# A narrower span of nodes per tile of edges in a graph-network kernel: 12 nodes in place of 16

## The reference

```
xs = s @ W1_s / sqrt(64);  xv = einsum('nmc,mk->nkc', v, W1_v) / sqrt(32)
w  = silu(edge_embed @ fc_w1 + fc_b1) @ fc_w2 + fc_b2          # 192 weights per edge
m0_a = w_ss * xs[src] * sh0          m0_b = w_vv * einsum('emc,ec->em', xv[src], sh1) / sqrt(3)
m1_a = (w_sv * xs[src]) x sh1        m1_b = w_vs * xv[src] * sh0
agg = segment_sum(msg, dst, num_segments=n) / sqrt(AVG_DEG)
out = agg @ W2 + own features @ Wsc, gated by silu, added to the node features
```

## Time and profile before

| | us |
|---|---|
| median of three runs | 550.05 |
| the profiled execution's own time | 550.69 |
| its span, first to last instruction | 549.0 |
| gathers (L535) issued from, to | 41.2 to 535.5 |
| PE busy (at a mean granted clock of 0.936) | 474.3 |
| POOL busy (gaps between gathers not counted) | 401.4 |
| DVE busy | 368.0 |
| ACT busy | 202.1 |

### The profile page before, as it was taken

How to read it: one execution, slowest core, us unless ns; L and a number is a source line. 1 busy time by engine, 2 the same in 40 slices (tenths; PEclk the granted TensorE clock), 3 DMA queues, 4 the chain that set the end, 5 groups by cost and what they waited for, 6 DMA issues and landing times.

```text
span 549.0 us, 16081 instructions
## 1 busy us (share of the span) xinstructions
PE 474.3 (86%) x5423; PEld 354.2 (65%) x5423; DVE 368.0 (67%) x1234; ACT 202.1 (37%) x412; POOL 401.4 (73%) x429
## 2 busy tenths in 40 slices
PE   6839778889898999989899899899899989899896
PEld 5735555667665766667576667666666756676675
DVE  7945575666677587667667666676577667667664
ACT  4654422333343334333334334343243334334331
POOL 7737777777777777777777777777777777777770
PEclk9978699899899799989989899899799989989998
DMA  9982222222222222222222222222222222222220
GB/s 223 393 259 71 69 71 71 64 67 80 76 74 68 76 72 69 74 76 76 66 76 76 72 66 74 77 67 75 76 72 68 73 76 73 69 76 76 65 75 24
DMA packets 35374, 48.06 MB, mean 88 GB/s; under 512 B 9748, under 2 KB 27955, under 8 KB 34843
## 3 DMA queue, kind: packets, MB, share of 16 engines
q0 software_dynamic: 19968, 34.11, 22.8%
q1 hardware_dynamic: 14977, 13.65, 8.4%
q10 hardware_dynamic: 410, 0.07, 0.1%
HBM read 39.60 MB, written 4.00 MB: 79 GB/s over the span
## 4 chain that ended last, share of the span: by engine, by line
POOL 56%; issue 19%; PE 11%; DVE 4%; DMA 1%; DVEq 1%; ACT 0%
POOL gath L535 56%; PE ps L824 3%; PE ps L834 2%; PE ps L811 1%; DMA gath<-table,src_sb 1%; DVE P L645 1%; PE ps L829 1%; PE ps L801 1%; PE ps L866 1%; DVE agg L683 1%; DVE raw_stats L713 1%; DVE P L640 0%; PE ps L859 0%; DVEq L668 0%; PE ps L830 0%
## 5 line engine op out<-in xcount | busy, mean ns | idle before, releaser
L535 POOL DMA_INDIRECT gath<-table,src_sb x392 | 375.2, 957 | 126.1 <-issue 117.0
L834 PE MATMUL ps<-S,P 128*64 128x32 f32 x2496 | 172.2, 228 | 0.0
L829 PE MATMUL ps<-S,P 128*64 128x48 f32 x832 | 121.2, 241 | 52.5 <-DVE agg L683 50.5
L824 PE MATMUL ps<-fc_sb,hid 128*128 128x384 f32 x416 | 161.4, 513 | 0.0
L834 PEld LDWEIGHTS ps<-S,P 128*64 128x64 f32 x2496 | 160.3, 143 | 0.0
L829 PEld LDWEIGHTS ps<-S,P 128*64 128x64 f32 x832 | 82.1, 139 | 114.4 <-DVE agg L683 74.2
L640 DVE TENSOR_TENSOR P<-ps,gath 128x512 f32<-128x512 f32 x103 | 71.2, 691 | 114.2 <-PE ps L824 66.2
L568 ACT ACTIVATE hid<-ps,fb_sb 128x256 f32<-128x256 f32 x104 | 49.2, 473 | 195.3 <-PE ps L811 133.6
L683 DVE TENSOR_TENSOR agg<-ps,agg 128x64 f32 x412 | 91.4, 222 | 27.3 <-DVE agg L683 0.3
L830 PE MATMUL ps<-S,P 128*64 128x16 f32 x832 | 105.5, 205 | 0.0
L645 DVE TENSOR_TENSOR P<-ps,gath 128x384 f32<-128x384 f32 x206 | 104.2, 548 | 0.0
(11 more groups left out here) (118 smaller groups left out, 347.5 us busy)
## 6 DMA issues: line engine op xcount, KB each, us to landing
gath<-table,src_sb POOLq DMA_INDIRECT x392, 2.5
agg<-zeros SPq DMA_DIRECT2D x4, 1024.0 KB
out<-res SPq DMA_DIRECT2D x24, 78.1 KB
x_sb<-x SPq DMA_DIRECT2D x5, 350.0 KB
emb<-emb_t SPq DMA_DIRECT2D x104, 16.0 KB
table<-prod SPq DMA_DIRECT2D x3, 420.0 KB
sh_sb<-sh_t SPq DMA_DIRECT2D x1, 840.0 KB
raw<-x,src_sb POOLq DMA_INDIRECT x24, 6.5
```

Of the source, the lines that this page charges most:

```text
L535: nc.gpsimd.indirect_dma_start(gath[:, u, j, :], None, table, bass.IndirectOffsetOnAxis(ap=src_sb[:, t:t + 1], axis=0)).then_inc(arrived, 16)
L824: ins = nc.tensor.matmul(w_ps(u)[:, 2 * g:2 * g + 2, 0:WN], hid[:, u % 2, g, :], fc2_sb[:, :, :], start=False, stop=True, skip_group_check ...
L829: nc.tensor.matmul(oj[0:64, :, 0:3], pj[:, 64:128], sj[:, :, 1:4], start=True, stop=True)
L834: ins = nc.tensor.matmul(oj[64:128, :, c:4:3 - c], pj[:, lo:lo + 64], sj[:, :, 0:2 + c:1 + c], start=(c == 0), stop=(c == NC - 1), skip_gr ...
```

## The change

A single constant is changed: the span of nodes that a tile of edges adds into.

```diff
--- before.py
+++ after.py
@@ -22,7 +22,7 @@
-WIN = 16
+WIN = 12
```

## The result

The changed kernel took 546.14 us (median of 6, 545.27 to 546.94) against 549.93 us (median of 6). The ratio is 0.993, with a 95% interval of 0.9918 to 0.9943. The forecast was 547.9, with a range from 546.2 to 550.0: the sign and the place were right, the gain of 3.8 us is 1.7 times the 2.2 forecast, and the time lies just under the range.

What follows compares the result with a forecast made beforehand. POOL's gathers were taken to bound the kernel. From 550.69 us profiled, 1.7 for the gathers and 0.5 for the tail leave 548.5; the same step from the 550.05 median gives 547.9, range 546.2 to 550.0 for 8 in 10.

Steps and rivals of the forecast that it cites:

- What bounds the kernel: Main part: POOL's gathers are the time, 392 x 1.246 = 488 us; POOL never really waits for products.
- How much goes: Gathers in the main part: shorter selectors and matches hold gathers up less, 1.7 us gained; bounds 3.7 gained, 2.3 lost.
- (a): POOL's gathers: each of 23 hold-ups stays, its selector ending 84 ns sooner relative to the gather; 1.8 us gained.
- (b): POOL's gathers: selectors fall on gathers at random; 25 hold-ups of 3.7 us become 19 of 2.2; 1.5 us gained.
- phase lock: Rival, main part: one selector per iteration settles just ahead of a gather; 1.8 us slower, 551.9 us; chance 3%.
- best case: Gains' bounds: all selector hold-ups gone, 3.7 us, plus 0.8 us in the tail, give 545.6 us.
- VectorE per quad: Main part: shorter match, selector and additions take 0.15 us less per quad on VectorE, hidden by the gathers.
- TensorE per quad: Scatter matmuls with fewer columns: 0.15 us less per quad; 0.21 by the slope, nothing if weight loads set the pace.
- Tail: After the last gather: scatter and VectorE work on the path get shorter, 0.5 us gained; bounds 0 and 0.8.
- No change: Rival: hold-ups do not shrink and only the tail's 0.5 us is gained, 549.6 us, from 548.95 up; chance 23%.
- Two passes: Rival: a tile spanning more than 12 nodes runs the main part twice, near 1050 us; chance under 1%.
- TensorE's clock: Rival: TensorE idles more, its granted clock falls and it no longer keeps up; about 580 us at 0.70; chance 2%.

Runs made afterwards that it cites:

- Sel_wide: Against the kernel before: span 12 in matmuls and additions, matches and selectors still 16 wide; ratio 0.9983.
- order16: The kernel before with the selector moved from after the first to after the third of a quad's additions; ratio 0.9963.
- order12: The changed kernel (span 12) with the selector after the third addition in place of the first; ratio 0.9968 to the kernel before.

## Why the prediction was right, and where it failed

**What bounds the kernel:** right. POOL's gathers set the pace, TensorE's 86% did not matter, and no gather waited for products. The mean gather fell to 948 ns (952 forecast), and the last one ended at 531.6 us (533.8).

**How much goes: wrong, and this is the failed step.** The term was 1.7 us, between (a), 23 hold-ups that stay and shrink by 0.08 us, and (b), a random phase with 19 left of 0.116 us. Measured: 7 (in the second profile 1) left, 3.0 us gone from selectors, 3.65 us in all from the gathers. Method (b) gave 25 and 3.7 us for the kernel before where the trace has 23 and 3.7; I took the match as support for a random phase, and the experiments don't bear it out. Sel_wide, order16 and order12 have 16, 12 and 19 where it says 25, 25 and 19; two profiles of one kernel have 23 and 24. The hold-ups of most kernels repeat in one slot of the loop instead, and the changed kernel's selectors lie elsewhere. Method (a) moved the selector's end by 84 ns relative to the gather; in the quad shown it moved by 0.22 us, since the instructions ahead of it moved too. I had that argument in the text, against the phase lock ("that slot waits for TensorE's weights, which come earlier now"), and did not carry it into the sum. The forecast's best case, 3.7 us from selectors and 0.8 from the others, held what was measured. That the new place is a cheap one was luck as far as the sum goes: nothing in it put the selectors there, and order12, with the same lengths, settled elsewhere.

**VectorE per quad:** right (0.15 us). **TensorE per quad:** wrong, 0.15 us taken, 0.01 us measured (none from start to start); the three forms' durations with 48, 32 and 16 columns (241, 228, 205 ns) had suggested a price per column that the pace of the stream doesn't have. The lower bound that I named, nothing, is nearer; that the weight loads set the pace, the reason beside it, is not tested.

**Tail:** taken 0.5, measured 0.8 us, within the bounds, for partly other reasons. In the first pair of profiles the products of the last whole quad start 2.50 us after their last gather was issued, where it was 2.75, and wait for its landing. The timeline of after:

```profile
526.87 0.95 POOL L535 DMA_INDIRECT gath<-table,src_sb  x1 [0.30 <-issue]
...
529.37 0.69 DVE L640 TENSOR_TENSOR P<-ps,gath 128x512 f32<-128x512 f32 x1 [1.72 <-DMA gath<-table,src_sb]
...
537.31 0.21 DVE L690 TENSOR_TENSOR agg<-ps,agg 128x48 f32 x1 [0.20 <-PE ps L834]
```

From there to the first of the last additions it is 6.73 in place of 6.94 us, as VectorE's columns say (0.22 forecast). The four last additions take 1.42 in place of 1.71, because the third no longer waits 0.4 us for TensorE. 0.25 + 0.21 + 0.29 = 0.75. The last of the three can't be put down to the change: in the second profiles the kernel before has no such wait (1.51) and the changed one has it (1.67), and there the tail is 13.0 against 13.5 us, the 0.5 forecast. The term that TensorE was to give, 0.75 us of shorter scatters, was nothing.

**Rivals.** No change: out, since the ratio's interval ends at 0.9943 and this rival began at 548.95, or 0.998; but its argument, that the phases move, is what acted, in the other direction. Two passes: none, the page has the same 392 gathers. TensorE's clock: the mean stayed at 0.936. Phase lock: the loop does lock, the mechanism was right, but into a place that costs less; that a place can also cost more is what order12 and span 20 show.

## What to carry to other kernels

Where one engine issues back to back and bounds the kernel, look at the spread of its identical instructions and at what runs beside the long ones: here 23 of 392 held 3.7 us, and an input moved to PSUM took them away. Before working out such a collision by chance, check in which slot of the loop it falls: here the engines wait for each other, the collisions kept to a slot, and what stands ahead of the colliding instruction moved them. A matmul's price per column should be read from the pace of the stream, not from the durations of single ones.

## What the runs showed of the hardware

A gather of 128 rows takes 946 or 949 ns (by execution) and is issued every 1.25 us. What delayed it is an instruction on VectorE with both inputs in SBUF that started at least 0.04 us ahead of it and still ran 0.125 us after its start: selectors that had ended 0.07 us in cost nothing, and neither did those that started after the gather (0.14 us after, gather from 100.67). Between the two, from some 0.03 us after the gather's start to 0.04 ahead of it, it is VectorE that waits, and not for the whole gather: such a selector ends where one started 0.03 us into the gather would. In the kernel before it takes 0.46 in place of 0.42 us, and the longest case is in order12, 0.42 in place of 0.36.

```profile
469.05 0.46 DVE L631 TENSOR_TENSOR S<-M,sh_sb 128x256 f32<-128x256 f32 x1
469.06 0.94 POOL L535 DMA_INDIRECT gath<-table,src_sb  x1 [0.30 <-issue]
```

Scatter matmuls with a quarter fewer columns (36, 24 and 12) and the same 64-column weight loads run at the same pace, 1.376 us a quad from the first start to the last, or 35 ns a matmul. The Trainium skill ("TensorE: Matmul & The Clock Gate", "Back-to-back issue gap") gives one price for all widths from 1 to 64 columns; by that rule, the trace agrees. The price that it states, about 25 ns, is not this stream's 35 ns, which has a weight load for each matmul.
